# Layer 0's rotary embedding from one projection of reordered rows, with its halves crossed by VectorE

## The chip, the core and the metric

The kernel runs on one core of a Trainium2 chip. The metric is the device time of one execution in microseconds (us), smaller is better; a measured time is the median of several executions. The profile of one execution comes beside it. Engines: TensorE (PE, its weight loads are PEld), VectorE (DVE), ScalarE (ACT), GpSimd (POOL), and SyncE (SP), which issues nearly all DMAs.

## The reference

Two transformer layers over x of 4 x 1024 x 128. Each has 16-head attention (head size 8) and, beside it on the same normalized input, a feed-forward part: eight experts with the best two of each token in layer 0, a gated one with 4-bit quantization in layer 1. Only layer 0's attention is touched here:

```python
def _apply_rope(x, cos, sin):
    even = x[..., ::2]
    odd = x[..., 1::2]
    return jnp.concatenate([even * cos - odd * sin, even * sin + odd * cos], axis=-1)
Q = _apply_rope(jnp.einsum('bsd,ed->bse', x, wq), cos, sin)
K = _apply_rope(jnp.einsum('bsd,ed->bse', x, wk), cos, sin)
V = jnp.einsum('bsd,ed->bse', x, wv)
scores = jnp.einsum('bhqd,bhkd->bhqk', Q, K) / math.sqrt(DIM_K)
weights = jax.nn.softmax(scores, axis=-1)
out = jnp.einsum('bhqk,bhkd->bhqd', weights, V)
x = x + attn(xn) + ffn(xn)          # layer 0, then layer 1 alike
```

## The kernel before

The work is cut by layer and batch element into eight **phases**, 0 to 7; phases 0, 1, 3 and 5 are layer 0, the others layer 1 (causal). A class `Plan` writes a list of 491 **slots**, and every engine's program is written by walking that list, so the order on each engine is fixed before the run.

A slot has up to one **step** (the scores of 4 heads for 128 keys and 512 queries: four products, four `exp` on ScalarE, L944, and in the next slot PV's four products into the bank `pO`) and up to one **quad** (the same scores the other way round, whose row maxima VectorE reduces, L1295 or L1299 where masked). Quads run 12 slots ahead of the steps: the first slots up to 38 hold quads and preparations alone. Beside them a slot carries up to three **X items**, each a product into one bank of a ring of seven PSUM banks, emptied by VectorE or ScalarE: `pj` (a projection), `lg` (router logits), `unit` and `y` (the two products of one of the 23 expert tiles of a phase), `fp` (the output projection), `gu`, `turn`, `down` (layer 1's feed-forward), and others. `put` sets an X item into the first slot with room, by costs in `HEAVY`; `banks` walks the slots with estimated durations (`ON_TENSOR`, `EMPTIES`) and gives every product the bank that it expects to be free first. All of this is made once, in Python.

Layer 0's projections are in `prepare`. For K and then Q, and for each half h of 512 tokens, there are two X items, `pj ... a` and `pj ... b`: the normalized tokens times the even rows of the weight, twice over (`wqa0`), and times the odd rows, twice over (`wqb0`). VectorE multiplies a by `rc` (cos, then sin; L1555) and b by `rs` (-sin, then cos; L1557). The sum of the two is made by POOL (L849; by VectorE in phase 0, L1599), and then the result is split in three bf16 parts: ScalarE copies the high part (`hi`), POOL subtracts it (`rem`, L853; VectorE in phase 0, L1486), ScalarE copies the middle part (`mid`), POOL subtracts again (`lo`, L857). SP stores the parts into `scratch` (L718) and loads them from there as `KX` and `QX` (L737, L739), laid out by head. Where POOL has layer 1's rounding in the same slots (`round`, L901 to L921), it comes first in the slot.

In phase 0 these steps stand alone at the start of the program (slots 5 to 8); those of phases 1, 3 and 5 lie in slots 72 to 75, 164 to 170 and 278 to 283.

SP issues in order, slot by slot: a tile's weights (`wt`: `w1r`, `w2r`, `b1r`; L762 to L767), its rows (`xs`, L776), its results (`ys`, L785), the loads of `KX` and `QX`, and after every `mtr` four small DMAs of the negated maxima (`QX<-mT`, L749). The weights of tile n+2 are issued behind the results of tile n.

## Time and profile before

| | |
|---|---|
| median of 3 executions | 1587.84 us (1585.6 to 1588.1) |
| the profiled execution | 1583.88 us, its span 1582.1 us |
| mean granted TensorE clock | 0.954 of full speed |
| busy share of the span | PE 91%, DVE 83%, ACT 72%, POOL 37% |
| the chain that ended last | PE 66%, DVE 11%, ACT 6%, issue 6%, POOL 5% |

Busy shares are averages over stretches with different bounds. A busy PE isn't a PE at its peak, since its products are pipelined. The chain of waits is followed back from the last instruction, each step to what released it. "Idle before" beside a row is the time for which the engine stood still just ahead of it, and what ended that.

### The profile page before, as it was taken

The numbers are of one execution on the slowest core, as the hardware profiler recorded it, in microseconds if no ns is written. First come the engines' busy times: TensorE is split into PE (matmuls) and PEld (weight loads), VectorE is DVE, ScalarE is ACT, GpSimd is POOL, SyncE is SP. The second block draws the span as 40 slices with busy tenths as digits, with TensorE's granted clock in tenths as the row PEclk, the third lists the DMA queues.
The fourth block names the chain that finished last, engine by engine and source line by source line (L and its number), as shares of the span: only waits on it lengthen the run. The fifth ranks groups of instructions, "written<-read, shape, count | busy, mean of one in ns | idle before, by whom it ended". The sixth has DMA issues, their size and how long they took to land.

```text
span 1582.1 us, 34276 instructions
## 1 busy us (share of the span) xinstructions
PE 1445.1 (91%) x10557; PEld 578.0 (37%) x10557; DVE 1318.5 (83%) x3386; ACT 1138.8 (72%) x2644; POOL 577.9 (37%) x531
## 2 busy tenths in 40 slices
PE   3878898999999999998999999999999988989996
PEld 1212343443333444433333344334344432323332
DVE  6969987878898788899889778889888889978991
ACT  2147777888688667778878856778888865776675
POOL 3002221202163545560242454641134474554453
PEclk8559999999899999999999999999999998999999
DMA  6301256433155262132351134123274110600000
GB/s 175 102 2 55 75 149 149 126 87 95 50 160 132 75 165 78 43 96 63 108 134 52 51 114 123 54 68 110 67 206 107 38 28 2 155 7 15 2 2 14
DMA packets 169833, 131.84 MB, mean 83 GB/s; under 512 B 31597, under 2 KB 143158, under 8 KB 169654
## 3 DMA queue, kind: packets, MB, share of 16 engines
q1 hardware_dynamic: 165562, 121.26, 28.8%
q0 software_dynamic: 4096, 8.40, 1.8%
q8 instruction: 91, 1.49, 0.4%
q14 instruction: 84, 0.69, 0.2%
HBM read 88.50 MB, written 40.50 MB: 82 GB/s over the span
## 4 chain that ended last, share of the span: by engine, by line
PE 66%; DVE 11%; issue 6%; ACT 6%; POOL 5%; SPq 3%; DMA 2%; DVEq 0%; ACTq 0%; POOLq 0%
PE ring L632 42%; PE pO L632 20%; DVE mparts L1295 6%; ACT PR L944 5%; PE ring L635 4%; SPq L718 1%; DVE junk L1299 1%; POOL bq L910 1%; ACT hid L1015 1%; POOL yq L915 1%; POOL yq L912 1%; POOL bq L901 1%; POOL rows_in L874 1%; DVE xr L1475 0%; DMA b1r<-in_b 0%
## 5 line engine op out<-in xcount | busy, mean ns | idle before, releaser
L944 ACT ACTIVATE PR<-ring 128x512 f32<-128x512 f32 (+3 forms) x1792 | 881.5, 556 | 298.9 <-PE ring L632 293.4
L1295 DVE TENSOR_REDUCE mparts<-ring 128x1 f32<-128x512 f32 x1280 | 807.0, 682 | 97.3 <-PE ring L632 91.6
L632 PE MATMUL ring<-QX,KX 50*128 50x512 bf16 (+3 forms) x1792 | 536.7, 366 | 75.0 <-ACT PR L944 34.5
L632 PE MATMUL ring<-KX,QX 48*128 48x512 bf16 (+3 forms) x1792 | 552.1, 374 | 14.3 <-DMA QX<-scratch 14.2
L632 PE MATMUL pO<-PR,VX 128*18 128x512 f32 (+3 forms) x3584 | 446.0, 570 | 7.3 <-ACT PR L944 5.4
L632 PEld LDWEIGHTS ring<-QX,KX 50*128 50x128 bf16 x1792 | 125.2, 94 | 597.5 <-issue 180.8
L1299 DVE CUSTOM_DVE_ANT_0 junk<-ring,diag 128x384 bf16<-128x384 f32 (+3 forms) x512 | 228.0, 486 | 44.8 <-PE ring L632 41.7
L901 POOL TENSOR_SCALAR bq<-bq 128x352 f32<-128x352 f32 (+1 forms) x40 | 47.2, 1179 | 308.4 <-ACT bq L1059 301.2
L874 POOL DMA_INDIRECT rows_in<-xn,at x64 | 62.9, 983 | 234.6 <-PE pO L632 133.2
L632 PEld LDWEIGHTS ring<-KX,QX 48*128 48x128 bf16 x1792 | 125.2, 94 | 33.5 <-DVE mparts L1295 17.6
L1015 ACT ACTIVATE hid<-ring,b1r 128x128 f32<-128x128 f32 x368 | 105.0, 369 | 23.1 <-PE ring L632 21.7
L632 PE MATMUL ring<-yx,w1r 128*128 128x128 f32 x736 | 106.1, 288 | 5.2 <-DMA b1r<-in_b 5.0
L890 POOL DMA_INDIRECT ra<-rows_out,at x64 | 61.9, 967 | 130.2 <-PE pO L632 97.1
L632 PEld LDWEIGHTS pO<-PR,VX 128*18 128x18 f32 x3584 | 60.6, 97 | 133.5 <-issue 87.5
L632 PEld LDWEIGHTS ring<-yx,w1r 128*128 128x128 f32 x736 | 90.0, 193 | 31.1 <-ACT PR L944 12.3
L632 PE MATMUL ring<-w2r,hid 128*128 128x128 f32 x736 | 97.5, 276 | 0.0
L632 PEld LDWEIGHTS ring<-w2r,hid 128*128 128x128 f32 x736 | 93.2, 197 | 0.9 <-DVE mparts L1295 0.5
L857 POOL TENSOR_TENSOR parts<-rb,parts 128x512 bf16<-128x512 f32 x30 | 34.8, 1159 | 117.6 <-ACT parts L638 117.6
L632 PE MATMUL ring<-identb,laterb 128*128 128x128 bf16 x512 | 74.0, 227 | 0.0
L910 POOL TENSOR_TENSOR bq<-hq,bq 128x352 f32<-128x352 f32 x64 | 59.9, 936 | 4.6
L915 POOL TENSOR_SCALAR yq<-yq 128x352 f32<-128x352 f32 (+1 forms) x40 | 60.2, 1506 | 3.3
L912 POOL TENSOR_SCALAR yq<-yq 128x352 f32<-128x352 f32 (+1 forms) x40 | 60.2, 1506 | 0.1
(165 smaller groups left out, 1314.9 us busy)
## 6 DMA issues: line engine op xcount, KB each, us to landing
w1r<-in_w SPq DMA_DIRECT2D x92, 256.0 KB
w2r<-in_w SPq DMA_DIRECT2D x92, 256.0 KB
scratch<-parts SPq DMA_DIRECT2D x48, 256.0 KB, 3.4
scratch<-parts SPq DMA_DIRECT2D x96, 128.0 KB, 2.4
KX<-scratch SPq DMA_DIRECT2D x64, 192.0 KB, 4.2
QX<-scratch SPq DMA_DIRECT2D x128, 96.0 KB, 4.4
xg<-rows_in SPq DMA_DIRECT2D x92, 64.0 KB
rows_out<-yx SPq DMA_DIRECT2D x92, 64.0 KB
```

The costliest lines, as they stand in the source:

```text
L632: return nc.tensor.matmul(dst, lhsT, rhs, start=start, stop=stop, **kw)
L635: return nc.tensor.transpose(dst, src, ident[0:src.shape[0], 0:src.shape[0]])
L874: nc.gpsimd.indirect_dma_start(xs[b % 2], bass.IndirectOffsetOnAxis(at[b % 2][:, c:c + 1], 0), xn[0][:, c % T, :], None).then_inc(s_sc[b], 16)
L890: nc.gpsimd.indirect_dma_start(yg[:, D * t:D * t + D], None, ys[b % 2], bass.IndirectOffsetOnAxis(at[b % 2][:, c:c + 1], 0)).then_inc(s_yg ...
L901: ins = nc.gpsimd.tensor_scalar(b_, b_, 1.0, None, ALU.max)
L910: ins = nc.gpsimd.tensor_tensor(b_, dst, b_, ALU.subtract)
L912: ins = nc.gpsimd.tensor_scalar(y, y, -1.0, 1.0, ALU.max, ALU.min)
L915: ins = nc.gpsimd.tensor_scalar(y, y, SHIFT, SHIFT, ALU.add, ALU.subtract)
L944: nc.scalar.activation(PR[:, n % 2, HALF * j + off:HALF * j + HALF], ring[plan.bank("E", k)][:, off:HALF], ACT.Exp, scale=SCALE).then_inc( ...
L1015: ins = nc.scalar.activation(hid[N % 2][:, P * fc:P * fc + P], src[:, P * fc:P * fc + P], ACT.Relu, bias=b1r[N % 2][:, fc:fc + 1])
L1295: v.tensor_reduce(dst, src[:, 0:w], axis=X, op=ALU.max).then_inc(s_mr, 1)
L1299: v.tensor_tensor_reduce(out=junk[k % 2][:, 0:w], in0=src[:, 0:w], in1=diag[:, HALF - w:HALF], scale=1.0, scalar=NEG, op0=ALU.add, op1=ALU ...
```

## The change

The two X items `a` and `b` of each half become one, `rope`. Its weight has the even rows of the projection in columns 0 to 63 and the odd rows in 64 to 127, so that one product gives the even outputs in partitions 0 to 63 and the odd ones in 64 to 127. VectorE makes three products of it: all partitions by `rc` (now cos, cos), and then each half of the partitions by `rs` into the other half of the second buffer. What follows (sum, `hi`, `rem`, `mid`, `lo`, stores) stays. The loads at the start change with it: six DMAs (four weights of Q and K, two tables) become eight, each of half a weight's columns or half a table's partitions. The planner gets costs for `rope`.

The words that came with the change also speak of PV's bank cleared by products of zeros in front of the first scores. The diff has nothing of this: `pO` is cleared by VectorE's memset in both kernels.

```diff
-ON_VECTOR = ("pj", "lg", "rt", "fin", "gu", "down", "fp")
+ON_VECTOR = ("pj", "rope", "lg", "rt", "fin", "gu", "down", "fp")
 HEAVY = {"unit": 24, "y": 6, "turn": 11, "xT": 10, "v": 11, "cT": 10, "xqT": 10, "of": 10, "wT": 10,
-         "pj": 11, "mtr": 8, "fin": 15, "gu": 8, "down": 5, "fp": 11, "lg": 5, "rt": 5}
+         "pj": 11, "rope": 30, "mtr": 8, "fin": 15, "gu": 8, "down": 5, "fp": 11, "lg": 5, "rt": 5}
...
-ON_TENSOR = {"unit": 13, "y": 14, "turn": 8, "xT": 11, "v": 13, "cT": 11, "xqT": 11, "of": 11, "wT": 10, "pj": 17,
+ON_TENSOR = {"unit": 13, "y": 14, "turn": 8, "xT": 11, "v": 13, "cT": 11, "xqT": 11, "of": 11, "wT": 10, "pj": 17, "rope": 17,
...
-EMPTIES = {"unit": 16.5, "y": 6.2, "turn": 7, "xT": 8, "v": 9, "cT": 8, "xqT": 8, "of": 8, "wT": 8, "pj": 10, "mtr": 4,
+EMPTIES = {"unit": 16.5, "y": 6.2, "turn": 7, "xT": 8, "v": 9, "cT": 8, "xqT": 8, "of": 8, "wT": 8, "pj": 10, "rope": 30, "mtr": 4,
...
                 if layer == 0:
-                    i = self.put(i + 1, ("pj", p, q, h, "a"), 3)
-                    i = self.put(i, ("pj", p, q, h, "b"), 3)
+                    i = self.put(i + 1, ("rope", p, q, h), 3)
...
-        loads_a = [(ident[:, :], ident_d), (W["wqa0"][:, :], wqa0), (W["wqb0"][:, :], wqb0), (rc[:, :], rope_c),
-                   (rs[:, :], rope_s), (W["wka0"][:, :], wka0), (W["wkb0"][:, :], wkb0)]
+        loads_a = [(ident[:, :], ident_d), 
+
+                   (W["wq0"][:, 0:P // 2], wqa0[:, 0:P // 2]), (W["wq0"][:, P // 2:P], wqb0[:, P // 2:P]),
+                   (rc[0:P // 2, :], rope_c[0:P // 2, :]), (rc[P // 2:P, :], rope_s[P // 2:P, :]),
+                   (rs[0:P // 2, :], rope_c[P // 2:P, :]), (rs[P // 2:P, :], rope_s[0:P // 2, :]),
+                   (W["wk0"][:, 0:P // 2], wka0[:, 0:P // 2]), (W["wk0"][:, P // 2:P], wkb0[:, P // 2:P])]
...
-                            ins = mm(dst[:, :], W["w" + "qk"[q] + part + str(layer)][:, :],
+                            ins = mm(dst[:, :], W["w" + "qk"[q] + str(layer)][:, :],
                                      src[:, HALF * h:HALF * h + HALF])
...
-                            if part == "a":
-                                ins = v.tensor_tensor(sums(n), src[:, :], rc[:, half], ALU.mult)
-                            elif part == "b":
-                                ins = v.tensor_tensor(left(n), src[:, :], rs[:, half], ALU.mult)
+                            if e[0] == "rope":
+
+                                low, high = slice(0, P // 2), slice(P // 2, P)
+                                count(v.tensor_tensor(sums(n), src[:, :], rc[:, half], ALU.mult))
+                                v.tensor_tensor(left(n)[low, :], src[high, :], rs[high, half], ALU.mult)
+                                ins = v.tensor_tensor(left(n)[high, :], src[low, :], rs[low, half], ALU.mult)
```

With fewer X items the plan puts other work elsewhere. The list still has 491 slots. In phase 1 the ropes stay in slots 72 to 75, and every `unit` and `y` of phase 0's tiles from tile 1 on comes one slot earlier. Phase 3's ropes go from slots 164 to 170 into 163 to 166, phase 5's from 278 to 283 into 278 to 281. From slot 186 to 277 and from 310 on both the items and which product follows which in a bank are those of before.

VectorE at the start of the program, phase 0's first two halves of K; `ra` and `rb` are the two buffers. Before:

```order
L1555 TENSOR_TENSOR ra<-ring,rc 128x512
L1557 TENSOR_TENSOR rb<-ring,rs 128x512
L1599 TENSOR_TENSOR ra<-ra,rb 128x512
L1555 TENSOR_TENSOR ra<-ring,rc 128x512
L1557 TENSOR_TENSOR rb<-ring,rs 128x512
L1599 TENSOR_TENSOR ra<-ra,rb 128x512
L1486 TENSOR_TENSOR rb<-ra,parts 128x512
```

And after:

```order
L1560 TENSOR_TENSOR ra<-ring,rc 128x512
L1561 TENSOR_TENSOR rb<-ring,rs 64x512
L1562 TENSOR_TENSOR rb<-ring,rs 64x512
L1604 TENSOR_TENSOR ra<-ra,rb 128x512
L1560 TENSOR_TENSOR ra<-ring,rc 128x512
L1561 TENSOR_TENSOR rb<-ring,rs 64x512
L1562 TENSOR_TENSOR rb<-ring,rs 64x512
L1604 TENSOR_TENSOR ra<-ra,rb 128x512
L1489 TENSOR_TENSOR rb<-ra,parts 128x512
```

Each half has one instruction more ahead of its sum; nothing else moved.

POOL in phase 3, from the first half's sum (`ra<-ra,rb`) on; `rb<-ra,parts` is `rem`, `parts<-rb,parts` is `lo`, the rest is layer 1's rounding. Before:

```order
L849 TENSOR_TENSOR ra<-ra,rb 128x512
L901 TENSOR_SCALAR bq<-bq 128x352
L907 TENSOR_SCALAR hq<-bq 128x352
L853 TENSOR_TENSOR rb<-ra,parts 128x512
L910 TENSOR_TENSOR bq<-hq,bq 128x352 x2
L857 TENSOR_TENSOR parts<-rb,parts 128x512
L849 TENSOR_TENSOR ra<-ra,rb 128x512
L912 TENSOR_SCALAR yq<-yq 128x352
L915 TENSOR_SCALAR yq<-yq 128x352
L853 TENSOR_TENSOR rb<-ra,parts 128x512
```

And after, up to the fourth half's sum:

```order
L852 TENSOR_TENSOR ra<-ra,rb 128x512
L856 TENSOR_TENSOR rb<-ra,parts 128x512
L852 TENSOR_TENSOR ra<-ra,rb 128x512
L904 TENSOR_SCALAR bq<-bq 128x352
L910 TENSOR_SCALAR hq<-bq 128x352
L860 TENSOR_TENSOR parts<-rb,parts 128x512
L856 TENSOR_TENSOR rb<-ra,parts 128x512
L852 TENSOR_TENSOR ra<-ra,rb 128x512
L913 TENSOR_TENSOR bq<-hq,bq 128x352 x2
L860 TENSOR_TENSOR parts<-rb,parts 128x512
L856 TENSOR_TENSOR rb<-ra,parts 128x512
L852 TENSOR_TENSOR ra<-ra,rb 128x512
```

Before, the second sum stands behind four roundings; now all four sums stand in front of where the third pair of roundings (L915, L918) begins.

SP in slots 83 and 84, up to the weights of tile 6 (`w1r`), from the second of twelve loads of `KX` and `QX` that follow `QX<-mT` there; `TENSOR_LOAD` and `ISA` read which expert it is. Before:

```order
L739 DMA QX<-scratch 48x2x512
L737 DMA KX<-scratch 48x2x1024
L739 DMA QX<-scratch 48x2x512 x3
L737 DMA KX<-scratch 48x2x1024
L739 DMA QX<-scratch 48x2x512
L737 DMA KX<-scratch 48x2x1024
L739 DMA QX<-scratch 48x2x512 x3
L785 DMA rows_out<-yx 128x128
L761 TENSOR_LOAD whose
L761 ISA x2
L762 ISA
L762 DMA w1r<-in_w 128x512
```

And after, all in slot 83:

```order
L752 DMA QX<-mT 1x8x128 x4
L740 DMA KX<-scratch 48x2x1024
L742 DMA QX<-scratch 48x2x512
L740 DMA KX<-scratch 48x2x1024
L742 DMA QX<-scratch 48x2x512 x3
L788 DMA rows_out<-yx 128x128
L764 TENSOR_LOAD whose
L764 ISA x2
L765 ISA
L765 DMA w1r<-in_w 128x512
```

Of the twelve loads that stood between `QX<-mT` and these weights six are left in front; the other six now come behind them.

## Rows read from the trace of the kernel before

**Rows 1.** The page: busy time by engine; the chain that ended last.

```profile
PE 1445.1 (91%) x10557; PEld 578.0 (37%) x10557; DVE 1318.5 (83%) x3386; ACT 1138.8 (72%) x2644; POOL 577.9 (37%) x531
...
PE 66%; DVE 11%; issue 6%; ACT 6%; POOL 5%; SPq 3%; DMA 2%; DVEq 0%; ACTq 0%; POOLq 0%
```

**Rows 2.** Stretches with projections of phases 1, 3, 5: busy by engine, clock.

```profile
core 0: us, PE busy (x) PEld busy (x) DVE busy (x) ACT busy (x) POOL busy (x), PEclk, DMA share, GB/s
...
200.00:212.00 12.00, 12.00 (x76) 4.98 (x69) 10.43 (x18) 8.93 (x18) 10.52 (x9) 1.00 0.38 119
...
525.00:535.00 10.00, 9.91 (x67) 3.96 (x66) 6.61 (x28) 7.37 (x18) 8.91 (x8) 1.00 0.02 4
...
900.00:910.00 10.00, 10.00 (x77) 4.39 (x73) 6.71 (x27) 6.22 (x16) 2.73 (x4) 1.00 0.25 68
```

**Rows 3.** Timeline, the start of the program: start us, us, instruction, idle before.

```profile
11.04 1.91 PEld L635 LDWEIGHTS ring<-ident,xn 128*128 128x128 f32 x8 [11.04 <-DMA s_wkb<-in_wkb]
...
14.77 1.02 PE L632 MATMUL ring<-flip,s_wkb 128*128 128x512 f32 x2
...
15.63 1.02 PE L632 MATMUL ring<-flip,s_wka 128*128 128x512 f32 x2
...
15.83 0.69 DVE L1557 TENSOR_TENSOR rb<-ring,rs 128x512 f32<-128x512 f32 x1 [0.17 <-PE ring L632]
...
17.16 0.68 DVE L1555 TENSOR_TENSOR ra<-ring,rc 128x512 f32<-128x512 f32 x1
...
17.77 0.68 DVE L1557 TENSOR_TENSOR rb<-ring,rs 128x512 f32<-128x512 f32 x1
...
18.48 0.69 DVE L1599 TENSOR_TENSOR ra<-ra,rb 128x512 f32<-128x512 f32 x1
...
36.92 5.58 PE L632 MATMUL ring<-KX,QX 48*128 48x512 bf16 x14 [14.20 <-DMA QX<-scratch]
```

**Rows 4.** Groups by form: a VectorE read of PSUM with half the elements.

```profile
L1299 DVE CUSTOM_DVE_ANT_0 junk<-ring,diag 128x256 bf16<-128x256 f32 x128 | 49.1, 421 | 12.4 <-PE ring L632 11.2
```

**Rows 5.** Timeline, phase 1's third and fourth halves (slots 74 and 75).

```profile
199.93 2.56 DVE L1295 TENSOR_REDUCE mparts<-ring 128x1 f32<-128x512 f32 x4
200.09 1.27 POOL L849 TENSOR_TENSOR ra<-ra,rb 128x512 f32<-128x512 f32 x1 [4.07 <-DVE rb L1557]
...
201.44 1.13 PE L632 MATMUL ring<-flip,s_wqa 128*128 128x512 f32 x2
...
201.46 0.63 ACT L638 ACTIVATE parts<-ra 128x512 bf16<-128x512 f32 x1 [0.67 <-POOL ra L849]
...
205.42 1.13 PE L632 MATMUL ring<-flip,s_wqa 128*128 128x512 f32 x2
```

**Rows 6.** Groups by form, POOL: mean ns is the number behind the bar.

```profile
L910 POOL TENSOR_TENSOR bq<-hq,bq 128x352 f32<-128x352 f32 x64 | 59.9, 936 | 4.6
...
L901 POOL TENSOR_SCALAR bq<-bq 128x352 f32<-128x352 f32 x32 | 35.2, 1099 | 237.3 <-ACT bq L1059 230.1 <-PE ring L632 7.0
...
L849 POOL TENSOR_TENSOR ra<-ra,rb 128x512 f32<-128x512 f32 x12 | 15.3, 1272 | 53.9 <-DVE rb L1557 53.9
...
L853 POOL TENSOR_TENSOR rb<-ra,parts 128x512 f32<-128x512 f32 x12 | 13.9, 1159 | 4.0 <-ACT parts L638 4.0
```

**Rows 7.** Timeline, loads of phase 1 and the weights of tile 6.

```profile
239.71 0.44 SPq L737 DMA_DIRECT2D KX<-scratch  x1
...
248.03 0.36 SPq L767 DMA_DIRECT2D b1r<-in_b  x1
...
252.03 2.05 PE L632 MATMUL ring<-yx,w1r 128*128 128x128 f32 x8 [4.69 <-DMA b1r<-in_b]
```

**Rows 8.** The stretches around that stall, one microsecond each; columns as in Rows 2.

```profile
250.00:251.00 1.00, 0.00 (x0) 0.00 (x0) 0.00 (x0) 0.00 (x0) 0.00 (x0) 0.64 1.20 310
...
257.00:258.00 1.00, 1.00 (x9) 0.53 (x6) 0.60 (x1) 0.57 (x2) 0.79 (x1) 0.95 0.00 0
```

**Rows 9.** The chain in order of time: the wait for phase 1's first rows.

```profile
369.46 2.45 DMA xg<-rows_in
```

**Rows 10.** The stretch around that wait; columns as in Rows 2.

```profile
360.00:380.00 20.00, 18.07 (x140) 6.09 (x138) 17.45 (x32) 16.58 (x38) 5.71 (x6) 1.00 0.31 87
```

More of the change, by code:

```diff
@@ L331, in number @@
                     self.mtrs[e[1:]] = len(self.mtrs)
-                if e[0] == "pj" and e[4] != "a":
+                if e[0] in ("pj", "rope"):
                     self.parts[e[1:4]] = len(self.parts)
-                    if e[4] == "b":
+                    if e[0] == "rope":
                         self.parts0[e[1:4]] = len(self.parts0)
@@ L383, in banks @@
                 work["P"].append((ON_TENSOR[e[0]], (), ("X", self.xs[e]), [("X", e)]))
-                first = (e[0] == "gu" and not e[3]) or (e[0] == "pj" and e[4] == "")
+                first = (e[0] == "gu" and not e[3]) or e[0] == "pj"
                 if first:
@@ L976, in _ @@
                     for e in s["xs"]:
-                        if plan.by[e][0] == "A" or (e[0] == "gu" and e[3] == 0) or (e[0] == "pj" and e[4] == ""):
+                        if plan.by[e][0] == "A" or (e[0] == "gu" and e[3] == 0) or e[0] == "pj":
                             act.wait_ge(s_x, filled(e))
@@ L983, in _ @@
                             copy(flip[:, HALF * h:HALF * h + HALF], src[:, :]).then_inc(s_freed["A"], 1)
-                        if e[0] == "pj" and e[4] == "":
+                        if e[0] == "pj":
                             _, p, q, h, _ = e
@@ L1595, in _ @@
                         ins.then_inc(s_freed["D"], 1)
-                        if e[0] in ("lg", "rt", "gu", "down", "fp") or (e[0] == "pj" and e[1] == 0 and e[4] == "b"):
+                        if e[0] in ("lg", "rt", "gu", "down", "fp") or (e[0] == "rope" and e[1] == 0):
                             dve.wait_ge(*freed(e))
-                        if e[0] == "pj" and e[1] == 0 and e[4] == "b":
+                        if e[0] == "rope" and e[1] == 0:
                             v.tensor_tensor(sums(n), sums(n), left(n), ALU.add).then_inc(s_sum, 1)
```

13 lines of the change are left out of this document (7 added, 6 removed).

## The prediction, on record before the changed kernel ran

> **What bounds the kernel now.** I read the page first: TensorE is busy for 91% of the span and carries 66% of the chain that ended last, VectorE is at 83% [rows 1]. Averages don't say what this change is worth, since it touches only four places, so I went by stretches of time. Next to the projections of phases 3 and 5 TensorE has no gap worth naming (9.91 and 10.00 of 10 us) while VectorE works for 6.61 and 6.71 [rows 2]: there TensorE is the bound, and each product taken from it pays. Next to those of phase 1 TensorE is full too, but VectorE is at 10.43 of 12 us [rows 2]: it has 1.6 us to spare, less than the change hands it. In phase 0 the projections stand alone in a serial start: the first scores begin at 36.92 us, after 14.20 us in which TensorE waited for the stored and reloaded parts [rows 3]. There VectorE's chain is the path and TensorE's time is free. Outside these places the two programs differ in placement (slots 76 to 185 and 284 to 309), and from slot 186 to 277 and from 310 on not at all.
>
> **The prices.** One projection of a half takes TensorE 0.86 us (14.77 to 15.63) [rows 3]. Sixteen of 32 go, so 12 in phases 1, 3 and 5 are worth 4 x 0.86 = 3.4 us to each. VectorE gets one instruction more per half. A whole one takes 0.68 to 0.69 us, and its neighbour starts 0.61 us after it (17.16 to 17.77), but 0.71 us after it where it has to wait for the one in front (17.77 to 18.48) [rows 3]. No row has VectorE on 64 partitions. The nearest row with half the elements, 256 columns instead of 512, takes 0.42 us [rows 4], but it has fewer columns and these have 512 still; I take 0.65 us, with 0.42 and 0.8 (0.61 for the new one, and 0.1 more for it and for the one behind it, should neither overlap) as ends.
>
> **Phase 0, the start.** Ahead of the third half's `rem`, on which the first loads wait, stand four halves, so four more instructions: 4 x 0.65 = 2.6 us. Against it, VectorE doesn't wait 0.17 us for a second product any more, about 0.2 us [rows 3]. The ends are 4 x 0.42 - 0.2 = 1.5 and 4 x 0.8 - 0.2 = 3.0. TensorE's first transposes waited until 11.04 us for the last of seven loads [rows 3]. There are nine now, with 128 KB less in all; an issue takes SP some 0.45 us, so the last may come 0.9 us later, or at the same time if the transfers and not their issue were late. I take no delay, 0.9 as the end. Sum: **+2.4 us**, from +1.5 to +3.9. VectorE's four weight steps behind it are ahead of the first scores by about the same as before, since both move together.
>
> **Phase 1.** The slots of the third and fourth half take 3.98 us (201.44 to 205.42) with TensorE full [rows 5]. Afterwards TensorE needs 3.1 us, but VectorE four row maxima (2.56 us [rows 5]) and three products (about 2.0 us), 4.6 us. It becomes the bound, +0.6 us in each of two slots. In the two slots ahead, TensorE's output projection still sets the pace and the full 0.86 us comes back in each, and the router's product behind leaves VectorE time to catch up. 2 x 0.6 - 2 x 0.86 = -0.5; with some of the catching up **-1.0 us**, from +1.2 (nothing comes back) to -3.4 (all four).
>
> **Phase 3.** TensorE gives back 3.4 us. But four halves that lay across seven slots now lie in four, and POOL has the rounding besides. From the first `rem` to the last sum it now has three sums (1.27 each), three `rem` and two `lo` (1.16 each; `lo` is the same kind of instruction) and four roundings (two of 1.10, two of 0.94) [rows 6]: 3.8 + 5.8 + 4.1 = 13.7 us, in three slots that offer about 12.6 us at the pace of TensorE. ScalarE waits for each of these results in order, and behind its wait stand the next `exp`s, for which PV waits. By the order I find it 2.6 us late at the end of slot 166 and 1.9 us more a slot later, 4.5 us in all, of which ScalarE's idle time (7.37 busy of 10 [rows 2]) takes about a third. **-3.4 + 3.0 = -0.4 us**, from -3.4 to +1.7 (the lateness rounded up to 5.1 and nothing hidden).
>
> **Phase 5.** The same 3.4 us, and no rounding from the third half on. But even in phase 1, ScalarE waited 0.67 us for POOL's sum [rows 5], and now two more VectorE products stand between the projection and the sum: up to 1.4 us later per half, four times. The output projection in the last of the four slots hides one or two of them. **-3.4 + 2.0 = -1.4 us**, from -3.4 to +4.2 (1.9 us paid at each of the four halves).
>
> **The weights of tile 6.** The largest stall that the change could move isn't a rotation. At 247.3 us TensorE wanted tile 6's weights and stood still for 4.69 us; the last of them had been issued at 248.03 and came 3.9 us later, because SP had first issued twelve loads of `KX` and `QX` from 239.71 on [rows 7]. The granted clock fell to half (1.2 of 2.4 GHz) within 250 to 251 us and was back at 257 [rows 8], so 5 us of work ran at half speed: 2.5 us more. Now six of the twelve loads come behind these weights, 6 x 0.47 = 2.8 us of SP's time. Tile 6 itself is wanted a slot earlier (3.2 us), but the tile items and the issues that follow them, this chain's included, come a slot earlier too. So the stall should shrink from 4.7 to about 1.9 us. A wait of 2.45 us elsewhere [rows 9] left the clock at full speed [rows 10], so the half-speed stretch should go with it: 2.8 + 2.5 = 5.3 at best. The next tile's weights now stand behind eight loads instead of four and may be late by up to a microsecond. **-4.0 us**, from -5.3 to +3.2 (the loads keep their pace and tile 6 is wanted 3.2 us earlier).
>
> **The sum.** 2.4 - 1.0 - 0.4 - 1.4 - 4.0 = -4.4 us. The profiled execution took 1583.88 us, 3.96 below the median of the three others, 1587.84, so the executions of one kernel differ by about as much as I forecast. Against the profiled one it would be 1579.5; against the median, which is what is compared, 1583.4 us. `pO` is cleared by the same memset in both kernels; its price is nothing.
>
> **The rivals.**
>
> *The stall stays.* Loads and weights share the same transfers, and if those and not SP's issues are what is late, tile 6 gains nothing or waits for tile 7 instead. For it: the DMA engines were at 1.20 of their share during the stall [rows 8]. The rest of the sum remains: -0.4, 1587.4 us. Chance 0.23.
>
> *The crossed products don't overlap.* In the rows a VectorE instruction overlaps its forerunner's end by 0.08 us unless it waits [rows 3]; the two that cross the halves, and the one behind them, may not. Then 0.3 us is added per half, 4 x 0.3 = 1.2 at the start and about 1.0 in phase 1: 1585.6 us. Chance 0.13. The Trainium skill speaks for this one (VectorE: DVE Perf Modes, Two Vector instructions with no wait between them): an instruction whose inputs or output start in another quarter of the partitions than the ones before is held until all earlier ones have finished. No row of this trace has such a crossing; by that rule the forecast would be 1585.6 instead of 1583.4.
>
> *Slower: POOL's conversions set the pace.* The mechanism is ScalarE's wait for `sum` and `rem`, in front of its `exp`s, in slots 163 to 168 and 278 to 281. It decides once ScalarE comes later than the roughly 1 us per slot that it has to spare. Price: all of the lateness, +1.7 in phase 3 and +4.2 in phase 5, and -1.0 at phase 1 becomes 0. With +2.4 at the start and -4.0 at the weights, +4.3: 1592.1 us. For it: POOL's list above is longer than its slots. Against it: ScalarE's idle time, and the long output projection in phase 5. Chance 0.18.
>
> *Far faster.* TensorE's products come back in full in phases 1, 3 and 5 (3 x 3.4), the stall and the slow clock go (5.3), the start costs 1.5: -14.0, 1573.8 us. For it: TensorE is full at all three places. Chance 0.10.
>
> The forecast itself has 0.32, and 0.04 is left for a reordered bank or a moved tile that stalls somewhere in slots 76 to 185, where some two thirds of the score banks are reused in another order. I can't price that from rows; both signs are possible.
>
> **Numbers.** From 1574 to 1593 us the range holds the forecast, both smaller rivals and the slower one with their spread, and about half of the far faster one. A change of 0.2%, 3.2 us, is about what a measurement of this kernel can tell from no change. Faster by more: 0.7 of the forecast, 0.2 of the staying stall, 0.4 of the crossed case and all of the far faster one, 0.22 + 0.05 + 0.05 + 0.10, with the rest 0.43. Slower by more: mostly the POOL case, 0.8 of it, 0.2 of the staying stall, and a little of the others: 0.22. Within: 0.35.
>
> **What would show it.** Right at the start: the first scores at about 39.3 us instead of 36.92, and VectorE's three products per half 0.6 to 0.7 us apart. In phase 1, VectorE without idle time over two slots, and TensorE waiting for banks that VectorE frees. In phases 3 and 5, ScalarE idle ahead of `parts` with POOL as the releaser, 1 to 2 us each, several times the present 0.67. At tile 6, a wait for `b1r` of about 1.9 us and a clock that stays at full speed. From slot 186 on, equal distances between equal items. The prediction is wrong if phases 3 and 5 together give back or cost more than 3 us, or if the wait for tile 6 is as long as it was or gone.

## The result, and the profile after

The changed kernel takes 1618.03 us (median of 4 executions, 1613.5 to 1621.69) against 1586.72 us for the kernel before (1583.19 to 1588.1). The ratio on record, 1.0182 with a 95% interval of 1.015 to 1.0213, is not the quotient of these two medians; by it the kernel is 29 us slower, by the medians 31 us. Forecast were 4.4 us less, 1583.4 us, and the measured time is outside the range, whose upper end was 1593. The profiled execution took 1617.85 us, its span 1616.1, 34.0 us more than that of before. Two executions further down, the profiled one of told_uncrossed (1611.4 us) and one of before beside before_later (1598.1 us), are in a slower state at a lower clock and are left out of the ratios and means (though not of the medians), and no trace of told_uncrossed is read.

The page of the changed kernel, busy time by engine and the chain that ended last, as in [rows 1] of before:

```profile
PE 1458.1 (90%) x10525; PEld 584.7 (36%) x10525; DVE 1330.6 (82%) x3402; ACT 1137.9 (70%) x2644; POOL 577.5 (36%) x531
...
PE 63%; DVE 15%; ACT 6%; issue 6%; POOL 5%; SPq 3%; DMA 2%; another core or an unknown queue 0%; DVEq 0%; ACTq 0%; POOLq 0%
```

TensorE has 32 instructions less and is busy for 13 us longer, and VectorE's part of the chain has grown from 11% to 15%. Fewer products that take longer in all point to the clock. To see where, I cut both spans at the first `exp` of the same slots: 50, 72, 86, 90, 162, 174, 278 and 290. Of before, the start, slots 72 to 86 (phase 1's ropes), 86 to 90 (tile 6), 162 to 174 (phase 3's), 278 to 290 (phase 5's); the columns are those of [rows 2], the last three being granted clock, DMA share and GB/s:

```profile
0.00:123.80 123.80, 84.65 (x309) 23.66 (x309) 95.31 (x202) 37.94 (x74) 13.56 (x24) 0.64 0.33 89
...
188.30:245.80 57.50, 57.50 (x389) 25.54 (x385) 48.05 (x118) 43.29 (x98) 14.11 (x12) 0.97 0.53 133
245.80:266.00 20.20, 15.51 (x108) 6.74 (x108) 12.14 (x27) 11.85 (x28) 2.96 (x3) 0.83 0.65 155
...
510.80:562.60 51.80, 50.50 (x391) 25.48 (x390) 35.98 (x125) 34.25 (x91) 24.24 (x22) 1.00 0.33 96
...
899.40:951.50 52.10, 50.00 (x385) 24.61 (x377) 38.19 (x142) 30.31 (x84) 24.04 (x22) 0.97 0.35 99
```

The same slots of the changed kernel:

```profile
0.00:119.40 119.40, 75.98 (x301) 20.42 (x301) 97.17 (x206) 37.79 (x74) 13.56 (x24) 0.67 0.36 92
...
183.90:250.40 66.50, 60.35 (x395) 26.28 (x393) 51.73 (x124) 44.28 (x102) 14.09 (x12) 0.90 0.49 131
250.40:263.80 13.40, 13.40 (x110) 5.97 (x102) 11.94 (x26) 11.56 (x28) 2.96 (x3) 1.00 0.65 185
...
512.30:579.60 67.30, 60.21 (x375) 29.27 (x367) 40.45 (x159) 33.97 (x89) 22.45 (x20) 0.77 0.30 85
...
920.10:979.40 59.30, 53.05 (x380) 27.70 (x383) 45.57 (x151) 30.86 (x84) 24.49 (x22) 0.88 0.41 110
```

The length of a stretch times (1 - clock) is what the half-speed clock cost in it, if all of its work hangs on TensorE and TensorE is never idle at half speed. It is an estimate, and the most that the clock can have cost:

| stretch | longer by | of which clock | rest | forecast |
|---|---|---|---|---|
| start to slot 50 | -4.4 | 39.4 - 44.6 = -5.2 | +0.8 | +2.4 |
| slots 72 to 86, phase 1 | +9.0 | 6.7 - 1.7 = +5.0 | +4.0 | -1.0 |
| slots 86 to 90, tile 6 | -6.8 | 0 - 3.4 | -3.4 | -4.0 |
| slots 162 to 174, phase 3 | +15.5 | 15.5 - 0 | 0.0 | -0.4 |
| slots 278 to 290, phase 5 | +7.2 | 7.1 - 1.6 = +5.5 | +1.7 | -1.4 |
| all the rest | +13.5 | | | 0 |

In the three stretches with ropes that is 26.0 of the 31.7 us. The rows show the rest without this estimate: TensorE's own idle time, length less busy, rose from 0 to 6.2 us in phase 1, from 1.3 to 7.1 in phase 3 and from 2.1 to 6.3 in phase 5. Over the whole span the same sum (mean clocks 0.939 and 0.954) makes 98.6 and 72.8 us, 26 of 34. The table's last line is spread: +3.7 in slots 90 to 162, +3.7 in 174 to 278, +6.1 behind 290, much of it where both programs are the same. The kernel loads_last, below, runs there from slot 290 on what before runs, and its profile has 643.5 us where before's has 630.6, so such a sum over long stretches is partly the chance of one execution. So is the start: up to slot 50 it took 117.8 to 124.2 us in the profiles of four other kernels with before's instructions there.

How TensorE's clock falls in phase 3. Six stretches of the changed kernel, columns as above:

```profile
520.00:524.00 4.00, 2.48 (x18) 1.66 (x15) 2.81 (x10) 1.91 (x5) 2.29 (x2) 0.95 0.02 4
524.00:528.00 4.00, 4.00 (x18) 0.40 (x16) 2.47 (x4) 2.13 (x5) 0.49 (x2) 0.63 0.39 117
...
536.00:540.00 4.00, 3.88 (x16) 1.53 (x16) 0.80 (x2) 2.70 (x8) 3.91 (x4) 0.65 0.01 1
...
544.00:548.00 4.00, 2.06 (x20) 0.60 (x18) 2.09 (x8) 0.65 (x3) 3.92 (x4) 0.93 0.74 235
548.00:552.00 4.00, 3.30 (x16) 3.30 (x17) 0.00 (x0) 2.06 (x6) 2.49 (x3) 0.50 0.79 213
...
568.00:572.00 4.00, 4.00 (x25) 1.77 (x24) 1.72 (x13) 1.74 (x4) 0.00 (x0) 0.58 0.29 76
```

TensorE is idle for 1.5 us of the first four, and 3.4 us at half speed (1.2 of 2.4 GHz) follow, from 523.6 to 527; the same comes again from 537.2 to 540.6. From 544 to 548 it is idle for 1.9 us while POOL works without a gap, and then the clock is at half from 547 to 571 us, though TensorE is full again from 552 on. Before, the same slots had no time at the lower clock.

Now the cause of such gaps. The timeline of the changed kernel in slots 74 and 75, phase 1's third and fourth half, where before had one half per 3.98 us [rows 5]:

```profile
199.82 2.07 PE L635 MATMUL ring<-flip,s_wq 128*128 128x512 f32 x2 [0.20 <-ACT PR L947]
...
201.93 0.69 DVE L1560 TENSOR_TENSOR ra<-ring,rc 128x512 f32<-128x512 f32 x1 [2.69 <-PE ring L635]
...
204.12 1.27 POOL L852 TENSOR_TENSOR ra<-ra,rb 128x512 f32<-128x512 f32 x1 [3.83 <-DVE rb L1562]
...
205.48 0.63 ACT L641 ACTIVATE parts<-ra 128x512 bf16<-128x512 f32 x1 [1.87 <-POOL ra L852]
206.02 1.06 ACT L947 ACTIVATE PR<-ring 128x512 f32<-128x512 f32 x2
...
206.65 2.08 PE L635 MATMUL ring<-flip,s_wq 128*128 128x512 f32 x2 [0.98 <-ACT PR L947]
```

This is a closed loop of 6.83 us: the rope's product (2.11 until VectorE starts, at half clock), three VectorE instructions (2.19), POOL's sum (1.36 until ScalarE starts), ScalarE's high part (0.54), the `exp` that was queued behind it (0.63), and then the next rope, which waits for that `exp`. It waits because the planner has put it into the bank of this slot's third or fourth score. In the plan of before no projection of slots 73 to 75 stands behind a third or fourth `exp`: they stand behind row maxima, and one behind a second `exp`. The planner reckons when an `exp` is over without knowing that the high part ahead of it waits for POOL, and with another number of products per slot the ring of seven banks came out differently. In the whole plan of the changed kernel twelve X items stand behind the third or fourth `exp` of a slot that has a high part in it, six of them ropes (slots 73, 74, 75, 164, 166 and 281); in the plan of before none does.

ScalarE's wait for POOL's sum, in the table of waits (us in total, times, longest), of the changed kernel:

```profile
ACT parts L641 <- POOL ra L852: 18.0, 11, 2.5
```

and of the kernel before:

```profile
ACT parts L638 <- POOL ra L849: 7.5, 11, 1.1
```

The start and tile 6, from the timeline of the changed kernel, to be read beside [rows 3] and [rows 7]:

```profile
18.52 0.69 DVE L1561 TENSOR_TENSOR rb<-ring,rs 64x512 f32<-64x512 f32 x1
19.22 0.68 DVE L1562 TENSOR_TENSOR rb<-ring,rs 64x512 f32<-64x512 f32 x1
19.94 0.69 DVE L1604 TENSOR_TENSOR ra<-ra,rb 128x512 f32<-128x512 f32 x1
...
38.04 7.37 PE L635 MATMUL ring<-KX,QX 48*128 48x512 bf16 x17 [18.62 <-DMA QX<-scratch]
...
248.26 1.13 PE L635 MATMUL ring<-yx,w1r 128*128 128x128 f32 x8 [1.71 <-DMA b1r<-in_b]
```

Here a VectorE instruction on 64 partitions takes as long as one on 128 (0.68 to 0.69 us), and the crossed ones start 0.70 to 0.72 us apart, where whole ones started 0.61 apart. The first scores come 1.1 us later than before, and the wait for tile 6's weights is 1.71 us instead of 4.69, with the clock at full speed behind it.

### The profile page after: what moved, and what is told of

Its sections match the earlier page's. It is cut to its first block, busy times and chain, and to the rows that moved or that the text cites. A ratio compares the mean times of both kernels' runs of the same rounds, so it can differ in the third digit from the quotient of the medians.

```text
span 1616.1 us, 34204 instructions
## 1 busy us (share of the span) xinstructions
PE 1458.1 (90%) x10525; PEld 584.7 (36%) x10525; DVE 1330.6 (82%) x3402; ACT 1137.9 (70%) x2644; POOL 577.5 (36%) x531
## 4 chain that ended last, share of the span: by engine, by line
PE 63%; DVE 15%; ACT 6%; issue 6%; POOL 5%; SPq 3%; DMA 2%; another core or an unknown queue 0%; DVEq 0%; ACTq 0%; POOLq 0%
PE ring L635 41%; PE pO L635 19%; DVE mparts L1298 8%; ACT PR L947 4%; PE ring L638 4%; DVE junk L1302 1%; SPq L721 1%; ACT hid L1018 1%; POOL ra L852 1%; DVE xr L1478 1%; DMA b1r<-in_b 1%; POOL bq L913 1%; POOL yq L918 1%; POOL yq L915 1%; DVE rb L1562 1%
## 5 line engine op out<-in xcount | busy, mean ns | idle before, releaser
L635 PE MATMUL ring<-QX,KX 50*128 50x512 bf16 (+3 forms) x1792 | 542.6, 369 | 82.1 <-ACT PR L947 40.9
L918 POOL TENSOR_SCALAR yq<-yq 128x352 f32<-128x352 f32 (+1 forms) x40 | 60.3, 1507 | 3.3
L915 POOL TENSOR_SCALAR yq<-yq 128x352 f32<-128x352 f32 (+1 forms) x40 | 60.1, 1502 | 0.1
```

The source lines that it names most:

```text
L635: return nc.tensor.matmul(dst, lhsT, rhs, start=start, stop=stop, **kw)
L915: ins = nc.gpsimd.tensor_scalar(y, y, -1.0, 1.0, ALU.max, ALU.min)
L918: ins = nc.gpsimd.tensor_scalar(y, y, SHIFT, SHIFT, ALU.add, ALU.subtract)
```

## The experiments

Each kernel was compared with the kernel before on the same chip; its median there lay between 1584.4 and 1590.1 us, so the ratios are what is to be compared; like that of the result, they are not the quotients of the medians. Two ratios must lie some 0.004 to 0.005 apart, 6 to 9 us, before their difference is clear of noise. Of the traces one stands for each kernel: the stretches of a trace are quoted where the edit acts, and they too have the chance of one execution in them. The table first, the kernels after it.

| kernel | median | ratio to before | 95% interval |
|---|---|---|---|
| changed | 1618.03 | 1.0182 | 1.015 to 1.0213 |
| spread | 1615.42 | 1.0177 | 1.0145 to 1.0209 |
| uncrossed | 1602.79 | 1.0079 | 1.0048 to 1.0109 |
| told | 1605.98 | 1.0104 | 1.0071 to 1.0137 |
| told_spread | 1606.8 | 1.0108 | 1.0066 to 1.0151 |
| told_uncrossed | 1591.86 | 1.0012 | 0.9989 to 1.0036 |
| later35 | 1593.51 | 1.0051 | 1.0024 to 1.0077 |
| later135 | 1593.31 | 1.0046 | 1.0014 to 1.0077 |
| two_packed | 1595.05 | 1.0049 | 1.0022 to 1.0076 |
| before_split | 1592.15 | 1.0059 | 1.0021 to 1.0097 |
| told_before | 1592.56 | 1.0012 | 0.9986 to 1.0038 |
| loads_last | 1592.51 | 1.0014 | 0.998 to 1.0048 |
| before_later | 1581.94 | 0.9974 | 0.9943 to 1.0005 |

**spread**: the changed kernel with its ropes of phases 3 and 5 in every second slot.

```diff
-                    i = self.put(i + 1, ("rope", p, q, h), 3)
+                    i = self.put(i + (2 if p >= 3 and (q, h) != (1, 0) else 1), ("rope", p, q, h), 3)
```

> The changed kernel, but in phases 3 and 5 a rope is set into every second slot (163, 165, 167, 169 and 278, 280, 282, 284) instead of every slot. Products and VectorE instructions are the same. Theory T (ScalarE waits in front of its exps for POOL's results of halves in adjacent slots, TensorE runs dry, and its clock then falls to half): the loss at steps 124 to 136 (15 us from the changed kernel's trace) and at steps 240 to 252 (7 us) goes nearly whole, 1592 to 1600 us instead of 1618. Rival D (the third VectorE product costs wherever it stands): four more of them per phase stay, so little comes back, 1610 us or more.

The total gave nothing back that can be measured, so theory T, which expected 18 us or more, fell. In the trace phase 3 got 7 us shorter (60.2 us for slots 162 to 174; its plan has no rope behind a third `exp` there any more) and phase 5 3 us longer. The reason is in the timeline of spread, in phase 5:

```profile
946.45 2.08 PE L635 MATMUL ring<-yx,w1r 128*128 128x128 f32 x8 [2.32 <-ACT PR L947]
```

A tile's product in slot 283 waits 2.32 us for an `exp` that stands behind a high part: in the plan it has the bank of slot 283's third score. The loop is the same, with another product in it. That turned the question from the slots to the banks.

**uncrossed**: the changed kernel with one VectorE product in place of the two crossed ones. It leaves out the crossing, so the rotation's second term takes the wrong rows.

```diff
-                                v.tensor_tensor(left(n)[low, :], src[high, :], rs[high, half], ALU.mult)
-                                ins = v.tensor_tensor(left(n)[high, :], src[low, :], rs[low, half], ALU.mult)
+                                ins = v.tensor_tensor(left(n), src[:, :], rs[:, half], ALU.mult)
```

> The changed kernel with VectorE's two crossed products of 64 partitions replaced by one uncrossed product of 128 (the rotation's second term then takes the wrong rows, so the values are others). Each half has one VectorE instruction less, everything else is in place. Rival D: all of the loss goes, and with half of TensorE's projections gone it is faster than before, 1580 us or less. Theory T: the chain per half is shorter by 0.7 us of some 6, the halves are still in adjacent slots, so only a part comes back, 1600 to 1612 us.

1602.79 us, within what theory T expected, but more than a part of the chain would suggest: the ratio falls by 1.0%. One VectorE instruction per half is worth some 16 us, where 16 of them last 16 x 0.7 = 11 us. And the kernel is still slower than before, with as many VectorE instructions and half the projections, so the instruction isn't all.

**two_packed**: the kernel before with the two projections of a half in one slot and the halves in adjacent slots.

```diff
-                    i = self.put(i + 1, ("pj", p, q, h, "a"), 3)
-                    i = self.put(i, ("pj", p, q, h, "b"), 3)
+                    i = self.put(i + 1, ("pj", p, q, h, "a"), 4 if p >= 3 else 3)
+                    i = self.put(i, ("pj", p, q, h, "b"), 4 if p >= 3 else 3)
```

> The kernel before, with its two projections per half and two VectorE products, but in phases 3 and 5 both projections of a half are set into one slot and the halves into adjacent slots (164 to 167 and 278 to 281), as the changed kernel has them. Theory T: the adjacent slots alone make it slower than before, by 8 to 20 us, with the same wait for POOL's results and a clock at half speed behind slot 165. Rival D: no change, 1587 us within 3.

8 us slower (the interval is 3 to 12), at the lower end of theory T. In slots 162 to 174 it takes 60.6 us against 51.8, at a mean clock of 0.89 (so 6.7 us of the 8.8 by the clock); phase 5 is as before. In its plan, too, the second projections of slots 165, 280 and 281 now stand behind third `exp`s. ScalarE's waits for POOL's sum did not grow (5.9 us in 11, 7.5 before), those for its `rem` did (12.7 us instead of 7.1).

**loads_last**: the kernel before with SP's loads of `KX` and `QX` last in each slot, phase 1's one slot later.

```diff
-                self.slot(i + (6, 8 if p else 11)[h] + g)["sp"].append(("load", p, h, g))
+                self.slot(i + (6, 8 if p else 11)[h] + g + (p == 1))["sp"].append(("load", p, h, g))
...
+            s["sp"].sort(key=lambda e: e[0] == "load")
             s["pool"].sort(key=lambda e: e[0] in ("scatter", "gather"))
```

> The kernel before, but SP issues the loads of KX and QX last in each slot, and those of phase 1 one slot later, so that tile 6's weights come ahead of eight of the twelve loads that stood in front of them. If SP's issues are what made tile 6's weights late, the wait of 4.7 us and the clock's fall behind it go: 5 to 7 us less, 1580 us. If the transfers themselves were late, the wait stays or moves to another tile: 1587 us.

No gain. Tile 6 now waits 1.31 us, but the next tile waits as tile 6 did:

```profile
258.68 2.05 PE L633 MATMUL ring<-yx,w1r 128*128 128x128 f32 x8 [4.92 <-DMA b1r<-in_b]
```

Eight of the twelve loads that stood in front of tile 6's weights now stand behind them, in front of tile 7's. In the changed kernel the stall really shrinks: from 235 to 300 us no tile but tile 6 waits for its weights. Its tiles themselves come in other slots. In later135, where the loads come three slots later and the tiles from slot 73 on, no wait for weights is left there.

**told**: the changed kernel, same instructions, same order; the planner's reckoning of the banks knows of two waits.

```diff
-                    work["A"] += [(9, (), None, ()) for e in s["act"]]
+                    work["A"] += [(9, [("sum", ("rope",) + e[1:])] if e[0] == "hi" else (), None,
+                                   [("hi", e[1:])]) for e in s["act"]]
...
-            work["A"] += [(2 if e[0] == "gates" else 7.5, (), None, ()) for e in s["late"]]
+            work["A"] += [(2 if e[0] == "gates" else 7.5, [("rem", e[1:])] if e[0] == "mid" else (), None, ())
+                          for e in s["late"]]
...
                     time[g] = clock[who]
+                    if g[0] == "done" and g[1][0] == "rope":
+                        time["sum", g[1]] = clock[who] + LAG + 18
+                    if g[0] == "hi":
+                        time["rem", g[1]] = clock[who] + LAG + 17
```

> The changed kernel with the same instructions in the same order on every engine; only the planner, when it chooses a bank for each product, now counts that ScalarE's high part waits for VectorE's products and POOL's sum, and the middle part for the first subtraction. 130 of 4119 products are put behind another earlier user of a bank, nearly all in slots 73 to 78, 164 to 168 and 280 to 284; the ropes of slots 73, 74, 75, 164, 166 and 281, or what stands beside them, no longer stand behind an exp that itself waits for the half before. Theory B (the loss is the closed loop rope, VectorE, POOL, ScalarE's high part, exp, bank, next rope, and the clock that falls behind its gaps): at steps 34 to 38, 126 to 132 and 241 to 246 most of the loss goes, ratio to before 0.998 to 1.006 instead of 1.018. Theory T (the work in adjacent slots is too much for POOL and ScalarE whatever the banks): ratio 1.012 or more.

The ratio falls from 1.0182 to 1.0104, some 12 us, by the choice of banks alone. That is between the two expectations (though the upper end of the interval, 1.0137, reaches theory T's): the loop is real, and it isn't all. The trace agrees: the three stretches with ropes take 64.1, 62.7 and 55.6 us, 10.7 less than in the changed kernel, and 21 more than before. TensorE in slots 74 and 75 of told:

```profile
199.86 1.13 PE L641 MATMUL ring<-flip,s_wq 128*128 128x512 f32 x2 [0.49 <-DVE mparts L1304]
...
201.65 0.69 DVE L1566 TENSOR_TENSOR ra<-ring,rc 128x512 f32<-128x512 f32 x1
...
203.08 0.68 DVE L1568 TENSOR_TENSOR rb<-ring,rs 64x512 f32<-64x512 f32 x1
203.79 2.48 DVE L1304 TENSOR_REDUCE mparts<-ring 128x1 f32<-128x512 f32 x4
...
204.54 1.12 PE L641 MATMUL ring<-flip,s_wq 128*128 128x512 f32 x2 [0.19 <-DVE mparts L1304]
```

A half now takes 4.68 us instead of 6.83, and the rope waits for a row maximum: VectorE, without a gap, is the bound, with 2.14 us of products and 2.5 of maxima.

**told_spread**: told and spread together.

> The same planner, with the ropes of phases 3 and 5 in every second slot. Theory B: as told or a little better, since the chain of each half also gets a slot to itself: 0.996 to 1.003 of before; the plain spread kernel (1.018) had failed because the unit in slot 283 stood behind a late exp. If instead each half's chain costs time wherever it lies, it stays at 1.012 or more.

As told, no better: the time shows nothing that distance between ropes is worth, with either choice of banks. It can't show less than some 9 us, though. In the trace the three stretches take 61.2, 57.9 and 54.5 us, 8.8 less than in told's, and as much is lost behind slot 290 (644.3 us against 636.3), where the two plans differ in one item alone. So distance may be worth something; this is open.

**told_uncrossed**: told with the edit of uncrossed.

> The told kernel with one uncrossed VectorE product in place of the two crossed ones (the second term of the rotation takes the wrong rows). The difference to told is the price of the third VectorE instruction once no bank closes the loop. Theory B: small, 12 x 0.7 us at most in phases 1, 3 and 5 and mostly covered, 1 to 5 us in all. Rival D (the third product is dear anywhere): 10 us or more, as between the changed kernel and uncrossed (15 us).

1591.86 us, 14 us less than told on the same chip, and level with before. Theory B expected 1 to 5 us for the third instruction and is wrong on this point; rival D's 10 us or more came true. The two effects add: banks 12 us (with three VectorE instructions) or 11 (with two), third instruction 16 us (old banks) or 14 (new), each to within some 7 us.

**told_before**: the same addition to the planner of the kernel before.

> The kernel before with the same addition to the planner: 74 of 4135 products stand behind another earlier user of a bank, the projections hardly among them. Theory B: before had no closed loop (its projections stood behind row maxima or early exps), so little changes: 0.997 to 1.002.

Nothing that can be measured, as expected: there was no closed loop to open.

**later35** and **later135**: told_spread, with the high part, the subtractions, the middle part and the store one slot later, in phases 3 and 5, or in 1, 3 and 5 (there the ropes are spread too). Of the two edits, the lines that set the high and the middle part; `w` is 1 in these phases and 0 elsewhere:

```diff
-                    self.slot(i + 1)["act"].append(("hi", p, q, h))
-                    self.slot(i + 1)["late"].append(("mid", p, q, h))
+                    self.slot(i + 1 + w)["act"].append(("hi", p, q, h))
+                    self.slot(i + 1 + w)["late"].append(("mid", p, q, h))
```

> As told_spread, and in phases 3 and 5 also the high part, the subtractions, the middle part and the store come one slot later, so that ScalarE reaches the high part more than a slot after VectorE's products and doesn't wait for POOL in front of its exps. Phase 1 stays as in told. Theory B (what is left of the loss, 12 us behind before in the bank-aware kernel, is the chain of each half standing in front of the exps, where VectorE's third product counts whole): the time in slots 164 to 170 and 279 to 286 falls to before's, ratio 1.000 to 1.005. Rival (work and not waits: VectorE, ScalarE and POOL are simply too full there): no better than told_spread, 1.009 or more.

> The same in phase 1 too: its ropes in slots 72, 74, 76, 78 and the results a slot later, tiles of phase 0 from slot 73 on, the loads of phase 1 three slots later. Theory B: another 2 to 4 us less than later35, 0.996 to 1.002 of before, and the fastest of the kernels with ropes. Against it: the loads of phase 1 come closer to the row maxima that need them in slot 90; if they are late, 3 to 6 us come back.

later35 gives back 9 us against told_spread (1.0108 to 1.0051, the difference just clear of noise). ScalarE's waits for POOL's sum are left in phase 1 alone:

```profile
ACT parts L649 <- POOL ra L860: 5.7, 4, 2.1
```

against 23.0 us in 12 in told_spread, the kernel it was made from. The expectation had two parts. The ratio just missed its upper end (1.0051 for 1.005); but the time in phases 3 and 5, which was to fall to before's, didn't:

```profile
507.80:564.00 56.20, 52.42 (x377) 26.45 (x369) 39.14 (x148) 34.16 (x87) 22.54 (x20) 0.88 0.28 83
899.80:955.10 55.30, 52.71 (x377) 25.69 (x369) 41.62 (x142) 30.12 (x84) 24.23 (x22) 0.85 0.28 82
```

That is 56.2 and 55.3 us for slots 162 to 174 and 278 to 290, where told_spread's trace has 57.9 and 54.5 and before's 51.8 and 52.1. By the traces, taking 17 us of waits away from in front of the `exp`s is worth about 1 us where they stood. So the gain isn't placed, and that the third instruction was dear because it lengthened this wait isn't shown: no kernel had the results later and the instruction out. later135 has no wait for the sum left, and slots 72 to 86 take 56.5 us (57.5 before, 66.5 in the changed kernel, 61.2 in later35), but the whole is the same within the interval. What keeps both 0.5% behind before is the clock, 0.85 to 0.88 in their phases 3 and 5, behind gaps on TensorE. In slots 162 to 174 of later35 its longest waits are two for an `exp`, 2.6 us in all; the rest of those gaps I didn't separate.

The clock of every execution is on record, not only of the profiled one, so the same estimate can be made with means over executions: span times mean granted clock, and what is left, span times (1 - clock), both in us and beside before's on the same chip.

| kernel | span x clock (before's) | half-speed clock (before's) |
|---|---|---|
| uncrossed | 1516.7 (1515.0) | 83.7 (73.1) |
| told | 1512.4 (1515.3) | 91.4 (71.5) |
| told_uncrossed | 1508.6 (1515.3) | 79.9 (71.5) |
| later35 | 1504.6 (1508.4) | 86.7 (74.3) |
| before_split | 1514.5 (1508.4) | 76.2 (74.3) |

By this estimate the kernels with ropes and mended banks have less to do than before, by 3 to 7 us, and lose it again to the clock. Of the third instruction's price between told and told_uncrossed 4 us (give or take 2) are work and 11 to 12 the clock; the 4 are within what theory B had expected. In before_split, the next kernel, it is the other way, 6 us work and 2 the clock.

**before_split**: the kernel before with VectorE's second product in two instructions of 64 partitions, not crossed.

```diff
-                                ins = v.tensor_tensor(left(n), src[:, :], rs[:, half], ALU.mult)
+                                v.tensor_tensor(left(n)[low, :], src[low, :], rs[low, half], ALU.mult)
+                                ins = v.tensor_tensor(left(n)[high, :], src[high, :], rs[high, half], ALU.mult)
```

> The kernel before with VectorE's second product of each half split into two instructions of 64 partitions each, which don't cross: same values, one instruction more per half, as the changed kernel has it, but two projections as before. It prices the third instruction alone. Theory B: VectorE's product is on the chain of the half, so 0.6 us each, 12 times in phases 1, 3, 5, mostly not covered where ScalarE waits for POOL, and 2.4 us at the start: 4 to 10 us, ratio 1.003 to 1.006, more if the clock falls behind it. If the instruction only costs when it crosses the halves of the partitions, 1.000 to 1.002.

1.0059, 9 us for the instruction (the interval is 3 to 15), at the upper end of theory B. ScalarE's wait for POOL's sum doubled, from 7.5 to 15.0 us. VectorE in phase 1 of before_split:

```profile
205.04 0.69 DVE L1555 TENSOR_TENSOR ra<-ring,rc 128x512 f32<-128x512 f32 x1
205.65 0.67 DVE L1558 TENSOR_TENSOR rb<-ring,rs 64x512 f32<-64x512 f32 x1
206.33 0.69 DVE L1559 TENSOR_TENSOR rb<-ring,rs 64x512 f32<-64x512 f32 x1
207.06 2.48 DVE L1295 TENSOR_REDUCE mparts<-ring 128x1 f32<-128x512 f32 x4
```

The first 64 partitions start 0.61 us behind the whole product; the upper 64 start 0.68 behind those, and the maxima 0.73 behind the upper ones. It takes 2.02 us from the first to the maxima, the crossed form 2.14 (201.65 to 203.79 above): the crossing itself costs VectorE 0.12 us a half, the instruction 0.7.

**before_later**: the kernel before, its results one slot later in phases 3 and 5, and phase 5's second projections in slots 279, 281, 283 and 285.

> The kernel before (two projections, two VectorE products per half) with the high part, the subtractions, the middle part and the store one slot later in phases 3 and 5, and the second projections of phase 5 in slots 279, 281, 283 and 285 (279, 281, 282, 283 before). In the kernel with ropes this distance gave back 9 us. Theory B: here the two projections already stand behind early users of their banks and ScalarE waited for POOL only 0.7 to 1.1 us at a time, at eight halves, so at most 3 to 5 us, ratio 0.997 to 1.000. If ScalarE's waits for POOL cost nothing in this kernel: 0.999 to 1.001.

0.9974, with 1.0005 in its interval: 4 us less or nothing, and both expectations allow it. The stretches that the edit touches are 1.0 us shorter in the trace. It is the only kernel of the study whose ratio is below 1, and it has no ropes.

## Why the prediction was wrong

**Start, +2.4.** The mechanism was right, the size too large: +1.1 at the first scores. The third half's `rem` came at 27.25 instead of 25.19 us, +2.06, but the first scores only 1.1 us later (38.04), since the loads behind it could be issued after 1.1 us more. Two sums that had taken 1.22 us each beside an instruction of POOL no longer overlap it and take 0.69. That the clock rose earlier within the start (-5.2 us) was in no term; two_packed, with before's start, has the same gain (117.8 us up to slot 50), so it isn't the change's.

**Phase 1, -1.0; here a step failed.** "The full 0.86 us comes back" in the slots where TensorE sets the pace supposes that TensorE can go on. It could not, since each rope stood behind an `exp` that waited for the half before. VectorE, forecast without idle time, stood still for 2.69 us ahead of a half. The step that gave +0.6 us a slot for VectorE was right in slot 74 as soon as the banks were: told has 4.68 us per half against 3.98. The term measured +9.0, of which 5.0 by the clock, and still +6.6 in told.

**Phase 3, -0.4, and phase 5, -1.4; here the costliest step failed.** The sign that was to show the prediction wrong, more than 3 us in these two phases together, came with 22.7. The wait was named: ScalarE idle ahead of `parts` with POOL as the releaser, 1 to 2 us each (18.0 us in 11 instead of 7.5). Its effect on TensorE was priced at 3.0 and 2.0 us; TensorE's idle time grew by 5.8 and 4.2 us, about twice that. And the waits were priced as time alone. At tile 6 I had counted 2.5 us for the clock behind a gap; in phases 3 and 5, where I forecast four gaps in a row, I counted none. By the estimate above the clock cost 15.5 and 5.5 us. The one row that spoke against such a fall was misread: the "wait of 2.45 us elsewhere" [rows 9] is a transfer in the chain. TensorE had other work beside it, and in the timeline of the kernel before it stood still for 0.91 us:

```profile
372.04 0.30 PE L635 MATMUL ring<-ident,xg 128*128 128x128 f32 x1 [0.91 <-DMA xg<-rows_in]
```

**VectorE's third instruction.** It was priced at 0.65 us and, in phases 3 and 5, as one part of 2.0 us. It takes 0.8 to 0.9 us of VectorE's time per half (2.14 us for three, where two with the same start took 1.20 to 1.32), and 14 to 16 us of the kernel's with ropes, 9 of the kernel before. With ropes that is about its whole length at all sixteen halves, though at the four of the start only 1.1 us reach the first scores. Why so much is open: it lies on the chain in front of the `exp`s, but later35 doesn't show that the wait there is the price. The rival with the crossed products had the size of the hold right, 0.3 us a half (three starts 0.1 us further apart); no run prices the hold alone, so its 2.2 us are neither shown nor refuted. The Trainium skill's rule (VectorE: DVE Perf Modes, Two Vector instructions with no wait between them) agrees with both traces: in before_split the lower 64, which start where the instruction ahead did, are not held, and the upper ones and the next are.

**The weights of tile 6, -4.0.** Right: the wait is 1.71 us, 1.9 were forecast, and the clock stayed up. The stretch is 6.8 us shorter. That it came so close has luck in it: told, with every engine's instructions in the same order, waits 2.35 us there, and its clock is at half from 249 to 252 us. loads_last showed the other half of that term, the next tile's wait, as larger than "up to a microsecond" when the loads alone are moved.

**What was left at 0.04**, "a reordered bank", was one of the two causes, 11 to 12 us, though most of it lies at the ropes themselves and not only in slots 76 to 185. The text called it impossible to price from rows. It could have been read from the plan: which products stand behind the third or fourth `exp` of a slot with a high part in it, where before has none.

The rival on the other side (POOL's conversions, 1592.1) named the right place and wait in phases 3 and 5, at +5.9 us where +22.7 were measured. It counted neither the banks nor the clock.

Shown by runs: that the banks are one cause (told against the changed kernel, told_uncrossed against uncrossed) and the third instruction the other (twice with ropes, and before_split), and that without both the kernel is level with before. Read from traces and granted clocks only: the clock's share, since no run held the clock up with the gaps in place. It also says where the gain of twelve projections less went: told_uncrossed has 6.7 us less of span times clock than before, and 8.4 us more at the lower clock. Left open: why the third instruction costs as much as it does, what distance between the ropes is worth, and which gaps hold the clock down in later35 and later135.

## What to carry to other kernels

When a result is awaited in front of other work in an in-order queue, look for a loop that comes back through the banks before counting what each engine saves. In such a loop every instruction counts with its length each time round, and time saved on an engine that waits in the loop brings nothing. A planner that assigns buffers by expected times must know the waits in every queue it models; when an edit changes how many products there are, compare who stands behind whom. And price a wait on TensorE twice: the gap, and the stretch at the lower clock that can follow several of them, which here was by estimate the larger part (26.0 of 31.7 us in the three stretches with ropes). Price it by TensorE's own idle time: a transfer's time in the chain isn't that.

## What the runs showed of the hardware

- A VectorE product of 64 partitions by 512 columns took 0.67 to 0.69 us, one of 128 partitions 0.68 to 0.69.
- In the changed kernel and in before_split, instructions whose partitions start elsewhere than those of the one ahead didn't overlap it: 0.68 to 0.73 us from start to start, against 0.61.
- A sum on VectorE that ran beside a tensor instruction of POOL took 1.22 us, and 0.69 us where it didn't.
- TensorE stood still for 0.7 to 1.9 us in each of five stretches of 4 us between 520 and 552 us, and the clock was at half for 24 us from 547 on, most of that with TensorE full. Before the long stretch it had twice been at half for 3.4 us.
- At tile 6 TensorE waited 1.71 us in the changed kernel and the clock stayed at 1.00; in told it waited 2.35 us, and the clock was 0.86 in the microsecond in which it went on and 0.50 in the three behind.
- The kernel before, unchanged, had medians from 1584.4 to 1590.1 us in these comparisons, and the same code from slot 290 on took 630.6 us in one profile and 643.5 in another.
